# The token steps project two groups of heads before the turns of both, with the router's product behind the turns

## What is computed

```python
q, k, v = x @ Wq, x @ Wk, x @ Wv            # 16 heads of 128; q and k through rmsnorm
scores = q @ k.T * scale + alibi_bias       # causal
y = rmsnorm(softmax(scores) @ v)            # per head
x1 = layernorm(x + y @ Wproj)               # y of 16 heads x 128 -> 512 channels
logits = x1 @ w_router                      # 8 experts, the two best are taken
h = square(relu(x1 @ w_fc[e]))
out = layernorm(x1 + sum_of_two(prob_e * (h @ w_proj[e])))
```

## Time and profile before

| | us |
|---|---|
| median of 3 runs | 1469.9 (1468.97 to 1472.49) |
| the profiled execution, its own time | 1471.34 |
| its span, first to last instruction | 1469.7 |
| attention stage | 0 to 966 |
| token steps | 967 to 1176 |
| slot steps and the end | 1176 to 1469.7 |

### The profile page before, as it was taken

How to read it: one execution, slowest core, us unless ns; L and a number is a source line. 1 busy time by engine, 2 the same in 40 slices (tenths; PEclk the granted TensorE clock), 3 DMA queues, 4 the chain that set the end, 5 groups by cost and what they waited for, 6 DMA issues and landing times. The chain is left out here.

```text
span 1469.7 us, 26490 instructions
## 1 busy us (share of the span) xinstructions
PE 1425.4 (97%) x7946; PEld 1204.1 (82%) x7947; DVE 772.0 (53%) x1813; ACT 727.4 (49%) x1633; POOL 414.4 (28%) x409
## 2 busy tenths in 40 slices
PE   7999999999999999999999999989999989999994
PEld 5888888888888888888888888878888877888883
DVE  6555655555555655555565565545555563333334
ACT  5565655655656555556565565622222223333334
POOL 1222121212122212122122121103233445335475
PEclk9999999999999999999999999999999999999998
DMA  5242333232323333223323335433348445675699
GB/s 179 75 128 93 107 97 124 86 114 85 115 93 107 109 113 102 98 92 108 103 97 126 95 107 177 145 112 137 130 124 215 133 173 208 244 263 194 209 205 236
DMA packets 86547, 200.45 MB, mean 136 GB/s; under 512 B 15856, under 2 KB 16496, under 8 KB 83184
## 3 DMA queue, kind: packets, MB, share of 16 engines
q1 hardware_dynamic: 75728, 149.66, 31.5%
q0 software_dynamic: 10784, 50.36, 12.2%
HBM read 160.05 MB, written 92.62 MB: 172 GB/s over the span
## 5 line engine op out<-in xcount | busy, mean ns | idle before, releaser
L375 POOL TENSOR_TENSOR small<-small,half 128x4 f32<-128x4 f32 x193 | 194.7, 1009 | 770.0 <-DVE small L404 770.0
L503 DVE CUSTOM_DVE_ANT_0 logit<-score_ps,bias 128x128 f32<-128x128 f32 (+3 forms) x256 | 124.8, 488 | 156.7 <-PE score_ps L629 117.7
L309 ACT ACTIVATE prob<-logit,small 128x128 f32<-128x128 f32 (+3 forms) x256 | 144.2, 563 | 119.1 <-DVE small L503 115.3
L642 PEld LDWEIGHTS y_ps<-vs,prob_t 128*128 128x128 f32 x1280 | 175.0, 191 | 20.4 <-issue 3.7
L642 PE MATMUL y_ps<-vs,prob_t 128*128 (+1 forms) x1280 | 184.8, 275 | 0.3 <-DVE x_now L408 0.3
L316 ACT ACTIVATE prob_t<-prob_ps 128x128 f32<-128x128 f32 (+3 forms) x256 | 111.5, 436 | 54.5 <-PE prob_ps L635 53.4
L870 ACT ACTIVATE yt_hi<-turn_ps,subln 128x512 fp32r<-128x512 f32 x60 | 41.0, 688 | 154.8 <-PE turn_ps L1164 154.8
L635 PE MATMUL prob_ps<-ident,prob 128*128 128x128 f32 x640 | 112.6, 274 | 2.4 <-ACT prob L309 2.2
L568 PE MATMUL k_ps<-w_hi,x_hi 128*128 (+1 forms) x256 | 103.8, 405 | 6.4 <-DVE w_lo L443 6.4
L568 PE MATMUL v_ps<-w_hi,x_hi 128*128 (+1 forms) x256 | 106.5, 416 | 0.0
L568 PE MATMUL v_ps<-w_hi,x_lo 128*128 (+1 forms) x256 | 106.3, 415 | 0.0
(11 more groups left out here) (245 smaller groups left out, 3406.8 us busy)
## 6 DMA issues: line engine op xcount, KB each, us to landing
slots_x<-in_zeros SPq DMA_DIRECT2D x64, 512.0 KB, 5.4
y_scratch<-x_now SPq DMA_DIRECT2D x65, 256.0 KB, 3.0
x_raw<-in_x_t SPq DMA_DIRECT2D x64, 256.0 KB, 2.9
slots_y<-in_zeros SPq DMA_DIRECT2D x64, 256.0 KB, 5.2
y_raw<-y_scratch SPq DMA_DIRECT2D x14, 1024.0 KB, 5.9
w_raw<-in_w_experts POOLq DMA_DIRECT2D x7, 2048.0 KB, 8.3
w_hi<-in_w_experts POOLq DMA_DIRECT2D x7, 2048.0 KB, 13.3
w_raw<-in_w_all SPq DMA_DIRECT2D x16, 768.0 KB, 6.5
```

What stands on the lines that cost most here:

```text
L309: nc.scalar.activation(prob[:, 0:width], logit[:, 0:width], ACT.Exp, scale=-1.0, bias=least[:, h:h + 1], accum_out=row_sum[:, (i % 2) * HG ...
L375: nc.gpsimd.tensor_tensor(r, ms, half[:, :], ALU.pow).then_inc(ready, 1)
L503: nc.vector.tensor_tensor_reduce(out=logit[:, 0:width], in0=score_ps[:, 0:width], in1=bias[:, h, T - width:T], scale=1.0, scalar=3e38, op0 ...
L642: mm = nc.tensor.matmul(y_ps[:, h * D:(h + 1) * D], prob_t[:, j * P:(j + 1) * P], one(vs[:, bass.ds(now, 1), j, h * D:(h + 1) * D]), start ...
```

## The change

Three streams are written in another order; no instruction of arithmetic is added or removed. On PE a step now has two halves. Each projects two groups, 24 products in a row, and then turns both groups. In the first half `turn_x1(s-1)` stands ahead of the two turns and `route(s-1)` behind them; in the second half `rank(s-1)` stands ahead of the turns. On ACT `second_weight` and the copy to `x1_t` (now `keep_x1_t`) go to the start of the step, ahead of `round_y(0)`, and the copy of the row tile (`keep_row`) stays behind `round_y(1)`. On DVE `split_y(0)` goes behind `layernorm` (and behind `choose_head` and `prepare_turns` in their steps), and `choose` goes ahead of `split_head` and `split_y(2)`. The slot steps' streams stay as they are.

```diff
--- before.py
+++ after.py
@@ -870,11 +870,17 @@
                 nc.scalar.activation(yt_hi[:, g, :], turn_ps[g][:, :], ACT.Copy, scale=subln[:, 0:1])\
                     .then_inc(yt_rounded, 1)
 
-            def keep_x1(t, b):
+            def keep_x1_t(t):
                 act.wait_ge(x1_turned, t + 1)
                 nc.scalar.activation(x1_t[:, :], x1_ps[:, :], ACT.Copy).then_inc(x1_t_ready, 1)
+
+            def keep_row(t, b):
                 out = x1[:, t, :] if isinstance(t, int) else one(x1[:, bass.ds(t, 1), :])
                 nc.scalar.activation(out, x1_now[:, b, :], ACT.Copy).then_inc(x1_kept, 1)
+
+            def keep_x1(t, b):
+                keep_x1_t(t)
+                keep_row(t, b)
 
             def second_weight(t, b):
                 act.wait_ge(gap_ready, t + 1)
@@ -883,12 +889,14 @@
                 nc.scalar.activation(second[:, b:b + 1], src, ACT.Exp).then_inc(second_ready, 1)
 
             def step(s, b, h):
+                if not before_step(s, 2):
+                    second_weight(s - 2, b)
+                if not before_step(s, 1):
+                    keep_x1_t(s - 1)
                 for g in range(NHG):
                     round_y(g, s * NHG + NHG + g + 1)
-                    if g == 0 and not before_step(s, 2):
-                        second_weight(s - 2, b)
                     if g == 1 and not before_step(s, 1):
-                        keep_x1(s - 1, 1 - b)
+                        keep_row(s - 1, 1 - b)
 
             token_steps(act, step)
             return second_weight, keep_x1
@@ -1136,7 +1144,6 @@
                     add_residual(s - 1, 1 - b, 16 * h + 16 * b)
                 if not before_step(s, 2):
                     place(s - 2, b, 32 * h - 32)
-                split_y(0, s * NHG + NHG + 1)
                 if not before_step(s, 2):
                     gates(s - 2, b)
                 if not before_step(s, 1):
@@ -1146,13 +1153,14 @@
                     choose_head()
                 if isinstance(s, int) and s == HEAD_STEP + 1:
                     prepare_turns()
+                split_y(0, s * NHG + NHG + 1)
                 split_y(1, s * NHG + NHG + 2)
-                split_y(2, s * NHG + NHG + 3)
+                if not before_step(s, 1):
+                    choose(s - 1)
                 if isinstance(s, int) and s in HEAD_SPLITS:
                     for c in HEAD_SPLITS[s][0::2]:
                         split_head(c)
-                if not before_step(s, 1):
-                    choose(s - 1)
+                split_y(2, s * NHG + NHG + 3)
                 split_y(3, s * NHG + NHG + 4)
 
             token_steps(dve, step)
@@ -1194,25 +1202,28 @@
                 nc.tensor.matmul(total_ps, ones_b[:, :], both[:, :], start=True, stop=True).then_inc(ranked, 1)
 
             def step(s, b, h):
-                for g in range(NHG):
-                    pe.wait_ge(yt_ready, s * NHG + g + 1)
-                    if not before_step(s, 1):
-                        mm = project(b, g)
-                        if g == NHG - 1:
-                            mm.then_inc(projected, 1)
-                    if g == 0:
+                def prepare_y(g):
+                    turn_y(w_raw[:, CT + g, :] if before_step(s, 1) else y_raw[:, 1 - b, g, :], g)
+
+                for half in range(2):
+                    for g in (2 * half, 2 * half + 1):
+                        pe.wait_ge(yt_ready, s * NHG + g + 1)
+                        if not before_step(s, 1):
+                            mm = project(b, g)
+                    if half == 0:
+                        if not before_step(s, 1):
+                            turn_x1(s - 1, 1 - b)
                         pe.wait_ge(y_loaded[1 - b], 16 * h + 16)
-                    turn_y(w_raw[:, CT + g, :] if before_step(s, 1) else y_raw[:, 1 - b, g, :], g)
-                    if not before_step(s, 1):
-                        if g == 1:
-                            turn_x1(s - 1, 1 - b)
-                        if g == 2:
-                            if before_step(s, 2):
-                                pe.wait_ge(const_loaded, 96)
-                                pe.wait_ge(set_up, 6)
-                            route(s - 1)
-                        if g == 3:
-                            rank(s - 1)
+                    elif not before_step(s, 1):
+                        mm.then_inc(projected, 1)
+                        rank(s - 1)
+                    prepare_y(2 * half)
+                    prepare_y(2 * half + 1)
+                    if half == 0 and not before_step(s, 1):
+                        if before_step(s, 2):
+                            pe.wait_ge(const_loaded, 96)
+                            pe.wait_ge(set_up, 6)
+                        route(s - 1)
 
             token_steps(pe, step)
             return project, turn_x1, route, rank
```

## The result

| | before | after |
|---|---|---|
| median | 1471.29 us (9 runs, 1468.97 to 1472.49) | 1476.52 us (9 runs) |
| profiled execution, its own time | 1471.34 | 1475.79 |
| its span | 1469.7 | 1474.1 |
| first product of step 1 to tile 14's rank | 220.32 | 224.33 |
| from there to the end of the span | 280.18 | 282.06 |

The changed kernel is slower. The ratio is 1.0035 with a 95% interval of 1.0024 to 1.0047, which is 5.2 us (3.5 to 6.9). Eight of its runs lie between 1473.44 and 1479.91; the ninth took 2030.13 at a granted clock of 0.65, was disturbed and is left out. The time lies inside the range that was given. The forecast that it would be within 0.3% of the kernel before, given 0.63, did not hold: it is 0.35% slower, just beyond that line (0.34 was given to this side), with an interval that has the line inside it.

The account below looks back on a forecast made before the run. PE, busy for 97% of the span, was taken to bound the kernel. The terms 1.3 + 1.0 - 0.3 + 1.7 gave +3.7 us, 1473.6 against the median of 1469.9, with a range of 1470.3 to 1477.0.

Parts of the forecast that it names:

- PE's own work: Token steps on PE: making four runs of turns into two saves 0, as switching between products and transposes costs nothing.
- The chain to x_now: DVE's chain through layernorm: normalised rows come late in steps 2, 4 and 6, not in 8 to 14; 1.3 us.
- B: Rival, slower: layernorm later than worked out in every step, so it and not PE sets the pace; 1476.5, chance 0.15.
- The router's operand: ACT's copy to x1_t comes late for route's weight load on PE: 0.07 in each of 14 steps, 1.0 us.
- Step 14: PE's rank no longer waits for choose behind split_head on DVE, since choose goes first: -0.3 us.
- D: Rival: the clock falls in every step, with transposes and router's product in a row; 21 us more, 1495, chance 0.03.
- Step 1, +1.7: Pipeline start: work left behind PE's wait for x_now, and a low clock until 986.3; ends -0.7 and +2.5.
- the credit of 1.5 us: Step 1: time the kernel before lost to 8 slow products at the low clock, subtracted from the changed kernel's cost.
- A: Rival: step 1's clock rises at 982.9 as before, costing +0.2 in place of +1.7; 1472.1, chance 0.22.
- C: Rival, faster: switches on PE do cost 0.08 each and nothing comes late; 1467.4, chance 0.05.

Follow-up runs that it names:

- the eight runs: The kernel before with each group's projection and turn cut in halves, eight runs of turns a step instead of four: median 1470.54 us, ratio 0.9998.

## Why the prediction came out as it did

**PE's own work, 0.** Right. Eight runs of turns take what four take. (Two sums of that paragraph are slightly off: with 0.233 the parts of a step make 14.24 and not 14.26, and 28 x 0.08 is 2.2 and not 2.4. Nothing hangs on either.)

**The chain to x_now.** Right as a chain: the starts of split_y(2) and add_residual are the forecast ones to 0.01, that of layernorm came 0.08 earlier, and steps 8 to 14 don't wait. Steps 2, 4 and 6 lost 0.51, 0.28 and 0.27 (1.06 us) where 0.57, 0.32 and 0.32 were forecast. These come to 1.2; the sum of 1.3 has a little for steps 3, 5 and 7 in it, which lost nothing. B, in which layernorm is late everywhere, is ruled out.

**The router's operand, 0.07 a step.** Right: 0.065 from the steps, 0.08 by the kernel that moves it back.

**Step 14, -0.3.** Right: -0.28.

So behind step 1 the sum was 1.3 + 1.0 - 0.3 = 2.0, and 1.6 was measured (202.6 us from there to tile 14's rank against 201.0, with the 0.86 taken into account).

**The clock in the other steps.** Right: it stays at 1.00, and D is ruled out, twelve turns in a row in each step or not.

**Step 1, +1.7: the term that was mis-sized.** The forecast picture is in the trace, point for point: 24 products done, one idle piece of about 4 us, no wait for y, a low clock up to 985.5 (forecast: about 986). Its size was not right in two places.

The first is the price of the low stretch in the changed kernel. The router's product took 1.62 at the low clock, where 2.4 for it and twelve turns together left it 1.1. And the low clock lasted 6.8 us in one profile only and 10.2 in the two others, where the turns run at half pace as well. The forecast amounts to 19.3 + 1.7 = 21.0; measured were 21.7, 22.6 and 23.0.

The second is the credit of 1.5 us for the low stretch that the kernel before had. It was read from one profile and taken for a part of that kernel. The second profile has the same waits and no low clock, and so has the one with choose first. On the mean of four profiles, two of them of kernels that differ a little, step 1 took 18.1 us and not 19.3, so 1.2 of the credit was not there to be given back.

Together step 1 costs 22.4 - 18.1 = 4.3 us, and the token steps 4.3 + 1.6 = 5.9. The medians differ by 5.2 and 4.9 us in the two comparisons. The profiles seem to have caught more of the low clock than the runs on the mean: in step 1 it lasts 1.7 us on the mean of the four and 9.1 on that of the three, 7.4 more, where all runs together have 5.5 more in the whole span. At the price above the 1.9 between them is 0.9 us (an estimate), and 5.9 less 0.9 is 5.0. In the two profiles first shown the difference is 4.0, close to the forecast 3.7, only by luck: that execution of before had the longest step 1 of the four.

**The rivals.** A, a clock that rises at 982.9 as before, is wrong in the other direction. The bound of +2.5 for step 1 was too low: against the 19.3 of the one profile it was +2.4, +3.3 and +3.7. C is ruled out by the eight runs. What decided whether this is a change within 0.3% or one beyond it was the one term whose row was a single event.

## What to carry to other kernels

Before a reordering is made to save switches, look whether a switch costs anything: compare a run of n with a run of 2n from start to start. What a reordering surely does is make some values early and others late, and that can be worked out from the rows to 0.1 us per step. The places where the pipeline is not yet full are to be costed apart: here a wait of 3 to 4.5 us on PE was followed by 3.4 to 10.2 us at half the clock each time, and a few instructions in another order there (nearly all of the 3.0 us here) gave more than the whole steady state could.

## What was unexpected on the hardware

- A low clock behind a wait is not a fixed price. Waits of 0.8 to 1.0 and then 1.8 to 1.9 us were followed by 3.4 us at 0.50 in one profile and by none in two others. One wait of 2.23, and one of 3.10 with one of 0.78 behind it, were followed by 3.4. Waits of 3.75 to 4.51 us were followed by 6.8 us in three profiles and by 10.2 in two. Late in the program the clock fell for 3.4 us behind a wait of 1.3 to 1.5 us in four of fourteen profiles, and not behind the same wait in the other ten.
- At a granted clock of 0.50 turns double too: twelve took 2.62 us and not 1.31. The router's product with its 8 columns took 1.57 to 1.62 us and not 0.89, and a product 0.43 and not 0.233.
- 34 turns in a row kept the granted clock at 1.00 as well as products did.
- Full-precision turns and products follow each other at their own paces, 0.109 and 0.233 us, with nothing in between.
